# Attention of a fused transformer block: shift rows copied one behind the other, denominator products together, VectorE's inverses between a group's maxima

## The reference, cut to what matters

```python
ctx     = _attn(qT, k, v)          # 16 heads, 4 batches, 512 queries, 496 keys
ctx_dca = _attn(qT, k_dca, v_dca)  # the same queries, the last 16 keys
ctx     = ctx + ctx_dca
def _attn(q, k, v):
    p = softmax(q @ k.T * SCALE)   # HD = 32
    return p @ v
```

## Time and profile before

| | us |
|---|---|
| median of 3 runs | 1060.17 (1059.81 to 1060.41) |
| profiled execution's own time | 1063.63 |
| its span | 1062.0 |
| attention: first S0 at 178.93, last scaled_main at 459.78 | |
| PE, DVE, ACT, POOL busy in 212.39 to 409.55 | 172.49, 155.27, 147.35, 136.16 of 197.16 |

### The profile page before, as it was taken

One profiled execution on the slowest core, in us unless ns is written; L12 is line 12 of the kernel. 1 busy time (PEld: TensorE's weight loads), 2 busy tenths in 40 slices (PEclk: granted clock), 3 DMA queues, 4 the chain that ended last, 5 costly groups with the idle time before them and its releaser, 6 DMA issues. The chain is left out here.

```text
span 1062.0 us, 17127 instructions
## 1 busy us (share of the span) xinstructions
PE 925.9 (87%) x5077; PEld 404.0 (38%) x5078; DVE 653.6 (62%) x1022; ACT 464.8 (44%) x844; POOL 614.1 (58%) x554
## 2 busy tenths in 40 slices
PE   1789894698988988879999389999999999999898
PEld 1345452111111211136644134454455444554343
DVE  5877774777877878447766145455545545443288
ACT  2365663667767777622353012322232223232440
POOL 0465556257667676443107488899899999000660
PEclk9899997599999999989999689999999999999899
DMA  7134445234444431123325754565556655444763
GB/s 262 35 103 132 137 135 168 70 134 175 146 170 166 142 110 62 51 72 134 132 83 219 278 159 159 186 198 176 177 180 198 187 175 171 119 119 179 279 198 139
DMA packets 104521, 162.31 MB, mean 153 GB/s; under 512 B 10904, under 2 KB 53912, under 8 KB 104080
## 3 DMA queue, kind: packets, MB, share of 16 engines
q1 hardware_dynamic: 90240, 115.13, 34.1%
q0 software_dynamic: 12896, 45.10, 12.2%
q10 hardware_dynamic: 1328, 1.36, 0.4%
HBM read 108.08 MB, written 53.48 MB: 152 GB/s over the span
## 5 line engine op out<-in xcount | busy, mean ns | idle before, releaser
L933 DVE TENSOR_REDUCE nm<-a_psS 128x4 bf16<-128x1984 f32 x64 | 142.7, 2229 | 63.8 <-PE a_psS L992 61.9
L890 ACT ACTIVATE p_t<-a_psT 128x512 f32<-128x512 f32 x256 | 138.9, 595 | 64.8 <-PE a_psT L1009 63.1
L843 POOL TENSOR_TENSOR p_sum<-p_t,p_t 128x512 f32<-128x512 f32 x64 | 81.4, 1273 | 93.6 <-ACT p_t L890 92.7
L1763 PE MATMUL e_psU<-w_exp,e_xT 128*128 x456 | 107.4, 386 | 7.6 <-issue 3.4
L1763 PE MATMUL e_psY<-w_exp,e_gT 128*128 x456 | 110.7, 379 | 0.9 <-ACT e_y L1704 0.9
L1763 PE MATMUL e_psG<-w_exp,e_uT 128*128 x456 | 106.5, 384 | 2.5 <-DVE e_uT L1718 2.5
L201 POOL TENSOR_TENSOR w_exp<-e_raw,w_exp 128x1024 f32 (+1 forms) x42 | 90.1, 2144 | 6.0 <-POOL e_raw L198 4.5
L1009 PE MATMUL a_psT<-q_stk,k_stk 98*128 98x512 f16 x256 | 85.8, 400 | 4.0 <-ACT p_t L890 1.5
L193 POOL TENSOR_TENSOR w_exp<-e_raw,ws_tile 128x1024 f32 (+1 forms) x42 | 80.2, 1909 | 6.1 <-DMA e_raw<-in_L_ffn_Wup_dram 5.2
L1690 ACT ACTIVATE e_gT<-e_psGT 128x512 f16<-128x512 f32 x38 | 22.7, 597 | 125.1 <-PE e_psGT L1753 125.1
L1745 DVE TENSOR_TENSOR e_g<-e_g,e_u 128x512 f32<-128x512 f32 x38 | 58.8, 1547 | 26.4 <-ACT e_g L1711 26.4
(11 more groups left out here) (317 smaller groups left out, 1792.8 us busy)
## 6 DMA issues: line engine op xcount, KB each, us to landing
xs_dram<-zero SPq DMA_DIRECT2D x38, 256.0 KB, 5.3
e_x<-xs_dram SPq DMA_DIRECT2D x38, 256.0 KB, 4.1
bias<-in_L_ffn_bup_dram SPq DMA_DIRECT2D x38, 256.0 KB, 3.7
bias<-in_L_ffn_bgate_dram SPq DMA_DIRECT2D x38, 256.0 KB, 3.9
ys_dram<-e_y SPq DMA_DIRECT2D x38, 256.0 KB, 4.0
q_dram<-q_st SPq DMA_DIRECT2D x24, 256.0 KB, 2.9
k_dram<-k_st SPq DMA_DIRECT2D x24, 256.0 KB, 3.7
q_stk<-q_dram SPq DMA_DIRECT2D x64, 96.0 KB
```

The lines of the kernel that those rows point to most:

```text
L843: pool.tensor_tensor(p_sum[:, w % SUMS, :], probs(w, 0), probs(w, 1), ALU.add).then_inc(s["sum_1"], 1)
L890: act.activation(probs(w, k), psT[:, k % 2], ACT.Exp, scale=SCALE / (QS * QS)).then_inc(s["exp"], 1)
L933: dve.tensor_reduce(nm[:, i, :, 0:1].rearrange("p h o -> p (h o)"), psS[:, :, 0:NMAIN], AX.X, ALU.max, negate=True)
L1763: ins = pe.matmul(dst[:, :], stationary, moving, start=(k == 0 and chunks[0] == 0), stop=(k == len(terms) - 1 and chunks[-1] == KD - 1))
```

## The change

The order in which PE, ACT and DVE take their pieces in `attend` is rewritten. No instruction is added or taken away, and every wait inside a piece stays as it was. M and S0 move from a period's end to its start, and T31 with them.

```diff
 ACT (L901 on)
             for p in range(PERIODS):
                 n = early_of(p)
+                if scored(p - 1):
+                    for h in range(G):
+                        max_row(G * (p - 1) + h)
+                pair(p - 2, TB - 1, 1)
                 for i in range(TB):
-                    for half in range(2):
-                        if scored(p - 1):
-                            exps(G * (p - 1) + i, 2 * half)
-                            exps(G * (p - 1) + i, 2 * half + 1)
-                        if i == 0 and scored(p - 1):
-                            max_row(G * (p - 1) + 2 + half)
-                        if i == TB - 1 and scored(p):
-                            max_row(G * p + half)
+                    pair(p - 1, i, 0)
+                    if i < TB - 1:
+                        pair(p - 1, i, 1)
 DVE (L966 on)
                 if scored(p):
                     maxima(p, 1)
+                if scored(gr):
+                    turned_sums(gr)
+                if scored(p):
                     maxima(p, 2)
                 if scored(gr):
-                    turned_sums(gr)
                     inverses(gr)
+                    scaled_dca(gr)
                 if scored(p):
                     maxima(p, 3)
                 if scored(gr):
-                    scaled_dca(gr)
                     main_inverse(gr)
                     scaled_main(gr)
```

More of the change, by code:

```diff
@@ L899, in hi_part, with pair @@
                 act.activation(oT_all[:, b, c, 0, :], r_main[:, gr % 2], ACT.Copy).then_inc(s["o_hi"], 1)
+            def pair(gr, i, half):
+                if scored(gr):
+                    exps(G * gr + i, 2 * half)
+                    exps(G * gr + i, 2 * half + 1)
             for p in range(PERIODS):
                 n = early_of(p)
+                if scored(p - 1):
+                    for h in range(G):
+                        max_row(G * (p - 1) + h)
+                pair(p - 2, TB - 1, 1)
                 for i in range(TB):
-                    for half in range(2):
-                        if scored(p - 1):
-                            exps(G * (p - 1) + i, 2 * half)
-                            exps(G * (p - 1) + i, 2 * half + 1)
-                        if i == 0 and scored(p - 1):
-                            max_row(G * (p - 1) + 2 + half)
-                        if i == TB - 1 and scored(p):
-                            max_row(G * p + half)
+                    pair(p - 1, i, 0)
+                    if i < TB - 1:
+                        pair(p - 1, i, 1)
                     if i == 1 and scored(p - 3):
@@ L1040, in dca @@
                 four(psX, lambda n: v_all[:, TB, n, :], gr, lambda n: probs(n, TB - 1), True, True).then_inc(s["dca_mm"], 1)
[L1042 to L1056, removed]
@@ L1058, in _, with turned_pair @@
-            scores(0, 0)
-            for p in range(PERIODS):
[L1060 to L1077, removed]
+            def turned_pair(gr, i, half):
+                if scored(gr):
+                    scores_t(G * gr + i, 2 * half)
+                    scores_t(G * gr + i, 2 * half + 1)
@@ new lines, in _ @@
+            for p in range(PERIODS):
+                new, now, old = p, p - 1, p - 2
+                if scored(now):
+                    max_rows(now)
+                if scored(new):
+                    scores(new, 0)
+                turned_pair(old, TB - 1, 1)
+                if scored(old):
+                    values(old, 0)
+                    sums(old)
+                if scored(new):
+                    scores(new, 1)
+                turned_pair(now, 0, 0)
+                if scored(old):
+                    third_sums(old)
+                turned_pair(now, 0, 1)
+                if scored(old):
+                    last_sums(old)
+                if scored(new):
+                    scores(new, 2)
+                if scored(old):
+                    values(old, 1)
+                turned_pair(now, 1, 0)
+                if scored(old):
+                    dca(old)
+                turned_pair(now, 1, 1)
+                if scored(new):
+                    scores(new, 3)
+                if scored(old):
+                    values(old, 2)
+                turned_pair(now, 2, 0)
+                if scored(old):
+                    values(old, 3)
+                turned_pair(now, 2, 1)
+                turned_pair(now, 3, 0)
```

## The result

The median went from 1060.17 us to **1063.99 us** (five runs each, 1062.54 to 1066.14 after): a ratio of 1.0044, 95% interval 1.0032 to 1.0057. It is slower, by 3.4 to 6.0 us, and outside the range given. The profiled execution after took 1062.54 us, a little less than the profiled one of before (1063.63). That is no contradiction: past attention the execution of before took 602.2 us of its span and that of after 595.3, for the same instructions. So attention is compared with attention. It ended with the scaled_main that starts at 459.78; now the same last scaled_main starts at 465.54, 5.8 us later.

The account below looks back on a forecast made before the run. Attention was bound by a 16.43 us loop of waits through PE, DVE and ACT, becoming 16.59 through ACT. Terms -3.5 + 1.9 - 0.9 + 2.2 = -0.3 us took 1060.17 to 1059.9, range 1056.8 to 1062.7.

Parts of the forecast that it names:

- The start: Attention's first groups, partly at half clock: sums of group 0 at 208.9 against 212.39, -3.5 us.
- The walk of the new loop: Steady attention period with a weight pass, sums to sums, added up from steps: 16.59 us against 16.43.
- its bracket of 1.06: Sign of being right: PE idle 1 us or more before sums in periods 2 to 13, naming ACT q_stk.
- F to S: PE's step from a wide product to an S product: taken as 1.00, bounds 0.88 and 1.00.
- S to T: PE's step from an S product to a turned pair: taken as 0.33, bounds 0.33 and 0.54.
- Rows stand 0.61 apart: ACT's rows directly behind one another: 0.59 long each and 0.61 apart, so no overlap.
- short-steps rival: Rows overlap like exponentials, -5.0, or F hides the following S's load, -3.4: 1054.9 or 1056.5; chance 0.24.
- That rival (1062.7): DVE holds S3 because turned_sums waits for last_sums: loop 16.8, 14 loops cost +2.8 more, 1062.7; chance 0.2.
- 12 x 0.16: Attention's periods 2 to 13, twelve loops with a weight pass, each 0.16 longer: +1.9 us.
- Two loops without a pass: Attention's two periods without a weight pass: 15.74 each, 31.5 against 32.42, -0.9 us.
- The end: From sums of group 14 to attention's last scaled_main: about 20.0 against 17.81, +2.2 us.
- the whole gain: DVE's loop is gone and every period takes 15.74: 14 x 0.69 = -9.7, with the ends 1050; chance 0.03.

Follow-up runs that it names:

- one F more: The changed kernel with one added F (a wide product, on constants) behind T21: ratio 1.0007, 1101.36 us against 1101.12 for the kernel before.
- the repeat: The changed kernel, unaltered, measured once more on another follow-up chip: ratio 1.0045, 1064.25 us against 1059.88 for the kernel before.
- either half alone: The changed kernel with DVE's old order: ratio 1.0201; the kernel before with DVE's new order alone: ratio 1.0261.
- row 3 late: The changed kernel with T31's exponentials put ahead of row 3 on ACT: ratio 1.0475, 1109.72 us.
- the hole alone: The kernel before with v0 moved behind S1 and v1 behind T01, no instruction added: ratio 1.0095.

## Why the prediction was wrong

- **The start** held: sums of group 0 at 209.04, forecast 208.9 (-3.35 for -3.5).
- **The walk of the new loop** held, at full clock: 16.57 for 16.59. Sums had its bracket of 1.06 that names ACT q_stk. Both steps that no row of before had came as taken: F to S 1.00 (225.80 to 226.80), S to T 0.32 (226.80 to 227.12) for 0.33. Rows stand 0.61 apart, four in 2.42. The Trainium skill, ScalarE: Activation LUTs, section What ACT_TABLE_LOAD costs, would have back-to-back ACTIVATEs overlap by about 93 ns. Four rows of 0.59 with nothing between took 2.42, so for these the trace does not agree, and neither half of the short-steps rival came true.
- **S3 was not held** by DVE. last_sums begins at 314.69 and the transpose at 315.83, 1.14 later where 1.1 was taken, and no S3 has a bracket that names DVE. That rival (1062.7) came near the result with a cause that did not occur.
- **The step that failed** is the term for the twelve loops with a weight pass, "12 x 0.16", +1.9. The 0.16 was right and the clock under it was not. The loop was summed from steps at full clock, and half clock was considered for the start only. The order set out with the change puts seven F, sums the first, with at most two short pieces between one and the next, and leaves T21, T30, M, S0 and T31 alone between v3 and v0; the prediction said that PE has "only T31 and v0 to cover the wait". It did not ask what the granted clock does in that hole. Measured, the twelve intervals cost +7.0. Of them the last ten, at 17.07 to 17.15, are 0.48 to 0.56 longer each than the 16.59 walked, together 5.0; the first two are 16.75 and 16.57.
- **Two loops without a pass** took 16.30 and 15.81, together 32.11 instead of 31.5: -0.3, forecast -0.9. The second is as walked (15.74). The last low stretch, from 410.8 to 414.3, reaches over the start of the first (413.2), and its sums take the same 0.5 more.
- **The end** took 20.22 from sums of group 14 to the last scaled_main, +2.4 for +2.2.
- Together -3.35 + 7.0 - 0.3 + 2.4 = +5.8, which is what attention lost. With all loops at full clock (16.57 for the last ten, 15.81 for the one at 413.2) it would have been about +0.1, inside the range: an estimate from these rows; the kernel with one F more, which has full clock in all loops, measured 1.0007.

The forecast median also carried over that the profiled execution of before stood 3.46 above its median. This was no part of attention, and the medians differ by 3.8 us (interval 3.4 to 6.0) where attention differs by 5.8 (5.3 in the repeat): the two agree within what a median tells here. In a rival that did not come, the whole gain, the sum is a little off: -3.5 - 9.7 + 2.2 from 1060.2 is 1049.2, not 1050.

## What to carry to other kernels

When an order gathers one kind of matmul together, look at what it leaves behind: a stretch of short products and short waits is a price of its own, in the granted clock, though no single wait in it is long. So walk the order twice, once for its waits and once for the longest time without the wide work, and put one of the movable products into that hole, which here cost one moved line and turned +0.4% into -0.6%. An engine order and its partner's order are one change: either half alone lost 2.0 to 2.6%.

## What the runs showed of the hardware that was not expected

- The clock fell with PE busy 2.24 of the 3.41 us before it and no wait over 0.56 us. In the kernel before it stayed full with PE busy 1.84 of 3.41 us, a wait of 1.57 among them. The Trainium skill, TensorE: Matmul & The Clock Gate, Part 1, says that the clock is set by how busy PE has been recently. The runs agree in direction (one F more and the clock stayed full), but neither the busy time in the rows nor any single wait announced the fall.
- Each low stretch in a loop was 3.41 us long (6.8 with row 3 late, but for its first). What lies in such a stretch sets its price: nothing for v0, which a wait covered, 0.50 for the half of sums, 1.27 in the loops with the hole alone, 2.8 with row 3 late.
- In after the low stretches began 17.07 us apart from the first on (240.18, 257.25, 274.32), while the loops came down to that spacing: 17.15, 17.11, 17.09, 17.08, then 17.07 for the last six without a change of 0.01. A loop longer than the spacing begins its sums later in the low stretch (2.19 us into it at 242.37, 2.35 at 327.87), so less of sums is stretched, until both are equal. So the 0.50 is what fits this spacing, and not a fixed price. With row 3 late the low stretches and the loops were both 20.48 apart, and with the hole alone 34.13 for two loops. What sets these spacings is not shown.
- A DVE transpose that waits for PE started 1.14 us after the F's first matmul, an F of 1.06; this hop (about 0.08 behind the end) had stood in no row of before.
